# One pool of eight PSUM banks, and the value products of a half step's last four key places moved next to those of the following half step

## The chip, the cores and the metric

The kernel runs on one core of a Trainium2 chip. The metric is the device time of one execution in microseconds; the median of three runs is compared. Its five engines (TensorE, VectorE, ScalarE, GpSimd and SyncE) each work through a queue of their own in order, and wait for each other by semaphores. TensorE multiplies matrices and writes its results to PSUM, which has eight banks here of 128 partitions x 512 float32; VectorE and ScalarE read them from there.

## The reference

The input is x of 8 sequences x 1024 tokens x 256 channels; there are 16 heads of 16 channels. What is computed:

```python
def attn(x):                      # relative positions clipped at +-64
    q, k, v = proj(Wq, bq), proj(Wk, bk), proj(Wv, bv)
    logits = einsum('bhqd,bhkd->bhqk', q, k) + einsum('bhqd,qkd->bhqk', q, embK[idx])
    w = softmax(logits)
    out = einsum('bhqk,bhkd->bhqd', w, v) + einsum('bhqk,qkd->bhqd', w, embV[idx])
    return out @ Wo.T + bo
def ffn(x):                       # weights quantized to -1, 0, 1 by a threshold
    return einsum('bsd,od->bso', x, ternary(weight) * alpha) + bias
x = x + layernorm(attn(layernorm(x)))
x = x + layernorm(ffn(layernorm(x)))
```

## The kernel before

**Work.** The heads are two groups of eight, a sequence is eight tiles of 128 queries: 8 x 2 x 8 = 128 steps, each of one tile of queries and eight heads. A step has two half steps of four heads each (`blk` 0 and 1), four steps are a quad, two steps a pair. For each step the stages are:

- `band_raw` (L902): products of the queries with the table of near positions, four matmuls into one bank. ScalarE copies the bank twice into `praw` (L1403, L1404); SyncE writes that to DRAM (`bs`) and reads it back skewed as `bands`.
- `row_max` (L919), eight times a step: scores for a pair of heads and half of the keys, in two banks, one for each of two heads (the sides). These matmuls have 48 or 51 rows, so two of them share the array as two row tiles. VectorE takes the maximum of either bank, with the band added (L1222) or without (L1216). `max_reduce` and `max_rows` (L929) turn the maxima, which go back by DMA as two more rows of the queries.
- `weights` (L946, with the band added by L950): the logits of four heads at one key place of 128 keys, transposed, in one bank. ScalarE takes the exponential (L1424). The eight key places of a half step are four of kind "X" (the nearest first; they go to `wl`, `wm` and the two of `wr`) and four of kind "Y" (the four of `wy`).
- `weighted` (L970): the products of the values with those weights. A visit is one kind of one half step: four key places x four heads, each with 17 output rows at one of four column tiles, all added up in one bank, `oacc`, over a pair of steps. `merge` (L1245) then joins `wl` and `wm` on VectorE. `out_copy` (L1432) copies `oacc` out after a pair.

Each quad `relative` (L982), `relative_sum` (L995) and `out_norm` (L1006) add the part of the relative values and normalise. The projections of the next sequence (`turn_x`, `project_q`, `far`, `project_k`, `project_v`; L865 to L892) and the output projection, norms and feed forward of finished tiles (`tail_...`, L1020 and L1034) are spread between the steps.

**Banks.** Three banks are the ring of the scores, two the ring of the logits, one is `oacc`, and two are `misc`, which all other stages share. A stage waits on TensorE until the reader of the bank's last user is done.

**Order.** Nothing is scheduled at run time. `timetable()` gives each stage a slot from the table `PLACES` (8 slots a step, 32 a quad; `near` and `rest` are the slots of kinds X and Y in a half step, `value_x` and `value_y` those of their visits). `with_banks()` goes through the slots in order, gives each stage that needs it the `misc` bank that is planned to be free first (`HOLD` is how long each is held, in slots), and moves a stage later where neither is. `order_of()` sorts them for each engine, with the lags of `LAG`; `misc_banks()` turns the plan into the semaphore values that TensorE waits for.

## Time and profile before

| what | before |
|---|---|
| median of three runs | 2571.98 us (2568.47 to 2572.31) |
| the profiled execution | 2569.9 us |
| its span in the trace | 2568.1 us |
| TensorE busy | 2413.4 us, 94% |
| VectorE busy | 2072.1 us, 81% |
| ScalarE busy | 1564.0 us, 61% |
| GpSimd busy | 955.9 us, 37% |
| mean granted TensorE clock | 0.979 |

Times count from the start of the span. A busy TensorE is one with a matmul in flight: matmuls overlap, and a row's length is that of one matmul from issue to end, so rates are read from the starts of rows. "PEld" are the weight loads, which run ahead of the matmuls. A wait stands at the engine that waited, with the instruction that released it.

### The profile page before, as it was taken

The page shows a single profiled execution, that of the slowest core. Times are in us where ns is not written, and L with a number is a line of the kernel's source. Part 1 is how long each engine was busy: PE and PEld are TensorE (multiplying, and loading weights), DVE is VectorE, ACT ScalarE, POOL GpSimd, SP SyncE. Part 2 cuts the span into 40 slices and gives each one's busy share as a digit, 9 for nine tenths or more (in the row PEclk, how much of TensorE's full clock was granted, in tenths as well). Part 3 has the DMA queues.
Part 4 walks back from the last instruction along what each step waited for, and adds up shares of the span by engine and source line. Part 5 has one row for each costly group of instructions (what it writes and reads, how often), then busy time and mean ns, then how long its engine had stood idle before and what let it go on. Part 6 is the DMA issues. An engine that isn't in the chain of part 4 may idle for free.

```text
span 2568.1 us, 101028 instructions
## 1 busy us (share of the span) xinstructions
PE 2413.4 (94%) x41858; PEld 1747.5 (68%) x41858; DVE 2072.1 (81%) x5306; ACT 1564.0 (61%) x2993; POOL 955.9 (37%) x2211
## 2 busy tenths in 40 slices
PE   5499999999999999999999999999999999999995
PEld 4266776777766776767776677676776777676673
DVE  4477779877888878887788878987788877888876
ACT  2266666666666666666666666666666666666651
POOL 3001534435343354425444253433534335442024
PEclk8599999999999999999999999999999999999998
DMA  6856675666746576565756667566774657756510
GB/s 162 228 155 180 184 195 146 167 176 193 205 138 174 165 205 185 148 193 152 206 153 176 184 182 194 147 168 174 199 201 139 173 163 203 192 145 189 153 42 29
DMA packets 696145, 434.20 MB, mean 169 GB/s; under 512 B 215846, under 2 KB 695430, under 8 KB 695558
## 3 DMA queue, kind: packets, MB, share of 16 engines
q1 hardware_dynamic: 695686, 427.75, 60.8%
q8 instruction: 329, 5.39, 0.9%
q14 instruction: 130, 1.06, 0.1%
HBM read 231.91 MB, written 194.92 MB: 166 GB/s over the span
## 4 chain that ended last, share of the span: by engine, by line
PE 54%; DVE 13%; issue 4%; ACT 3%; POOL 1%; DMA 0%; SPq 0%; DVEq 0%; ACTq 0%; POOLq 0%
PE logitsT L946 13%; PE oacc L970 12%; PE scores L919 7%; PE logitsT L950 6%; DVE junk L1222 4%; DVE maxes L1216 4%; PE misc L1034 3%; PE misc L875 3%; PE misc L995 2%; PE misc L892 2%; PE misc L902 1%; ACT wr L1424 1%; PE misc L982 1%; DVE stats L1092 1%; PE misc L1006 1%
## 5 line engine op out<-in xcount | busy, mean ns | idle before, releaser
L946 PE MATMUL logitsT<-qs,ks 98*128 98x128 bf16 (+1 forms) x8192 | 915.7, 221 | 21.8 <-ACT wr L1424 8.8
L1222 DVE CUSTOM_DVE_ANT_1 junk<-scores,bands 128x512 bf16<-128x512 f32 x988 | 679.5, 688 | 216.1 <-PE scores L919 66.7
L1424 ACT ACTIVATE wy<-logitsT 128x512 f32<-128x512 f32 x1024 | 581.4, 597 | 332.3 <-PE logitsT L946 321.1
L946 PEld LDWEIGHTS logitsT<-qs,ks 98*128 98x128 bf16 (+1 forms) x8192 | 562.4, 99 | 274.9 <-issue 150.4
L1216 DVE TENSOR_REDUCE maxes<-scores 128x1 f32<-128x512 f32 x1024 | 656.5, 682 | 93.8 <-PE scores L919 92.5
L919 PE MATMUL scores<-mks,mqs 48*128 48x256 bf16 (+6 forms) x3712 | 448.5, 289 | 36.8 <-DVE maxes L1216 12.6
L1424 ACT ACTIVATE wr<-logitsT 128x512 f32<-128x512 f32 x512 | 305.3, 596 | 200.2 <-PE logitsT L946 191.6
L950 PE MATMUL logitsT<-ident,bands 128*128 128x128 f32 x2048 | 410.6, 278 | 0.0
L1453 POOL TENSOR_SCALAR rs<-rs 128x1 int32<-128x1 int32 (+1 forms) x217 | 48.6, 224 | 803.3 <-DVE rs L1097 793.8
L950 PEld LDWEIGHTS logitsT<-ident,bands 128*128 128x128 f32 x2048 | 293.2, 143 | 20.6
L1458 POOL TENSOR_SCALAR rs<-rs 128x1 f32<-128x1 f32 x744 | 282.7, 383 | 64.9
L970 PE MATMUL oacc<-wy,vs 128*17 128x128 f32 (+1 forms) x9216 | 275.2, 262 | 4.5 <-ACT wy L1424 4.0
L919 PEld LDWEIGHTS scores<-mks,mqs 48*128 48x128 bf16 (+1 forms) x3712 | 138.9, 94 | 196.9 <-DVE maxes L1222 30.2
L1424 ACT ACTIVATE wl<-logitsT 128x512 f32<-128x512 f32 x256 | 158.6, 619 | 154.3 <-PE logitsT L950 152.5
L1463 POOL TENSOR_SCALAR rs<-rs 128x1 f32<-128x1 f32 x744 | 219.6, 298 | 66.1
L970 PEld LDWEIGHTS oacc<-wy,vs 128*17 128x17 f32 x9216 | 206.2, 97 | 53.1 <-issue 34.7
L1403 ACT ACTIVATE praw<-misc 128x512 f32<-128x512 f32 x256 | 154.7, 604 | 40.3 <-DMA bs<-praw 32.5
L1245 DVE COPY_PREDICATED wm<-later,wl 128x512 f32<-128x512 int32 x224 | 171.1, 764 | 0.0
L1424 ACT ACTIVATE wm<-logitsT 128x512 f32<-128x512 f32 x256 | 152.9, 597 | 24.6 <-PE logitsT L950 3.8
L970 PE MATMUL oacc<-wr,vs 128*17 128x128 f32 (+1 forms) x4608 | 159.3, 261 | 0.0
L1404 ACT ACTIVATE praw<-misc 128x512 f32<-128x512 f32 x256 | 157.5, 615 | 0.0
L902 PE MATMUL misc<-bandtab,qs 96*128 96x128 bf16 x1024 | 100.3, 220 | 20.3 <-ACT praw L1404 14.5
(147 smaller groups left out, 2991.3 us busy)
## 6 DMA issues: line engine op xcount, KB each, us to landing
bs<-praw SPq DMA_DIRECT2D x256, 512.0 KB, 4.6
bands<-bs SPq DMA_DIRECT2D x224, 512.0 KB, 4.5
ks<-kd SPq DMA_DIRECT2D x64, 384.0 KB, 4.9
qs<-qd SPq DMA_DIRECT2D x112, 192.0 KB
bands<-bs SPq DMA_DIRECT2D x128, 128.0 KB, 3.3
mks<-kd SPq DMA_DIRECT2D x128, 96.0 KB, 3.8
qd<-qparts SPq DMA_DIRECT2D x60, 192.0 KB, 2.6
kd<-kparts SPq DMA_DIRECT2D x60, 192.0 KB, 2.6
```

Source lines behind the costliest of these rows:

```text
L919: mm = e.matmul(scores[(u + side) % NSCORE][:, c % 512:c % 512 + length], mqs[i][HALF * side:HALF * side + depth, p, :], kk[HALF * side:HA ...
L946: mm = e.matmul(lt[:, j * P:(j + 1) * P], kk[0:depth, SLOT[HB * blk + j], kt * P:(kt + 1) * P], qs[i][0:depth, SLOT[HB * blk + j], :], sta ...
L950: mm = e.matmul(lt[:, j * P:(j + 1) * P], band[v % BRING][:, j, c * P:(c + 1) * P], ident[:], start=False, stop=True, is_transpose=True, s ...
L970: mm = e.matmul(oacc[32 * j:32 * j + VW, o0 + q0:o0 + q1], vs[m_ % VRING][:, int(right), kt, h, :], src, start=first and c == 0, stop=True ...
L1216: e.tensor_reduce(top, sc[:], AX.X, ALU.max).then_inc(row_maxed, 1)
L1222: e.tensor_tensor_reduce(junk[:], sc[:].rearrange("p (a c) -> p a c", a=2), banded, 1.0, LOWEST, ALU.add, ALU.max, top).then_inc(row_maxed, 1)
L1245: e.copy_predicated(right, mask.bitcast(I32), left).then_inc(merged, 1)
L1403: e.activation(dst[:, :, 0:P], src, ACT.Copy)
L1404: e.activation(dst[:, :, P:WIN], src[:, :, P - 1:P].broadcast_to([P, HB, P]), ACT.Copy).then_inc(praw_ready, 1)
L1424: e.activation(dst, src, ACT.Exp).then_inc(exp_ready, 1)
L1458: op = e.tensor_scalar(rs[k][:, 3, x:x + 1], rs[k][:, 2, x:x + 1], rs[k][:, 0, x:x + 1], rs[k][:, 2, x:x + 1], ALU.mult, ALU.mult)
L1463: op = e.tensor_scalar(rs[k][:, 2, x:x + 1], rs[k][:, 3, x:x + 1], 1.5, rs[k][:, 2, x:x + 1], ALU.add, ALU.mult)
```

## The change

- All eight PSUM banks become one pool, `bank0` to `bank7`. The scores (two banks at a time), the logits and the accumulation of the values take theirs from it as the other stages do. `with_banks()` plans them: a stage gets the bank that is planned to be free first; the second side of the scores is held 1.1 slots longer (`HOLD_NEXT`); the bank of the values is held from a pair's first visit to its `out_copy`. TensorE's waits are on the reader of the bank's last user, whichever that is.
- The visit of kind Y of a half step moves from slot 4.12 to slot 5.78, next to the visit of kind X of the following half step (3.5 + 2.3 = 5.8).
- A visit signals after each key place, not once; an exponential that overwrites a buffer waits for that place alone, and `merge` for the first two.
- At the start all eight banks are cleared by VectorE, where it was `oacc` alone.
- Some places, lags and holds have other numbers. The second half's band is now read back ahead of the first's.

```diff
-NLOG, NMISC, NSCORE = 2, 2, 3
+NBANK = 8
...
- 'half': 3.55,
+ 'half': 3.5,
...
- 'near': (0.0, 0.76, 0.72, 0.98),
- 'rest': (1.76, 2.1, 2.5, 2.77),
+ 'near': (-0.38, 0.76, 0.72, 0.98),
+ 'rest': (1.86, 1.98, 2.5, 2.77),
  'value_x': 2.3,
- 'value_y': 4.12,
+ 'value_y': 5.78,
  'merge': 3.2,
- 'out_copy': 7.74,
+ 'out_copy': 9.48,
...
+        if stage == "weighted" and k[0] // 2 in sums:
+            banks = sums[k[0] // 2]
+        elif stage == "out_copy":
+            banks = sums[k[0]]
+            until[banks[0]] = slot + HOLD[stage]
...
-                bank = until.index(min(until))
-                if until[bank] > slot:
+                banks = tuple(sorted(range(NBANK), key=lambda x: until[x])[:2 if stage == "row_max" else 1])
+                free = max(until[x] for x in banks)
+                if free > slot:
...
-         'out_norm': 0.7,
+         'out_norm': 0.24,
...
+HOLD_NEXT = 1.1
+HOLD = {'weighted': 0.0,
+ 'out_copy': 1.0,
+ 'row_max': 0.45,
+ 'weights': 0.45,
...
- 'band_raw': 0.2,
+ 'band_raw': 0.23,
...
-                            pe.wait_ge(row_maxed, u + side - NSCORE + 1)
-                            mm = e.matmul(scores[(u + side) % NSCORE][:, c % 512:c % 512 + length],
+                            pe.wait_ge(*frees[side])
+                            mm = e.matmul(banks[side][:, c % 512:c % 512 + length],
...
-                    pe.wait_ge(exp_ready, block + 1 - NLOG)
+                    pe.wait_ge(*free)
...
-                    mm.then_inc(pvX if kind == "X" else pvY, 1)
+                        mm.then_inc(pvX if kind == "X" else pvY, 1)
...
-            e.memset(oacc[:], 0.0).then_inc(oacc_zeroed, 1)
+            for bank in misc:
+                op = e.memset(bank[:], 0.0)
+            op.then_inc(banks_zeroed, 1)
...
-                    dve.wait_ge(pvX, value["pvX", s, blk])
+                    dve.wait_ge(pvX, value["pvX", s, blk] - 2)
...
-                        act.wait_ge(done, value["pv" + kind, (v - 1) // 2, (v - 1) % 2])
+                        act.wait_ge(done, value["pv" + kind, (v - 1) // 2, (v - 1) % 2] - 3 + c % 4)
```

What stands in a row on TensorE, in the middle of the program. First the kernel before: the end of a half step's key places, its X visit, and the turning of the row maxima.

```order
L946 MATMUL logitsT<-qs,ks 128x128 x8
L919 MATMUL scores<-mks,mqs 128x128 x4
L919 MATMUL scores<-mks,mqs 128x256 x2
L946 MATMUL logitsT<-qs,ks 128x128 x4
L970 MATMUL oacc<-wl,vs 17x128 x4
L970 MATMUL oacc<-wm,vs 17x128 x4
L970 MATMUL oacc<-wr,vs 17x128 x8
L929 MATMUL misc<-ident,negmax 8x128
L946 MATMUL logitsT<-qs,ks 128x128 x8
```

Some ten rows further on, the same kernel's Y visit, between the scores and the next key places:

```order
L919 MATMUL scores<-mks,mqs 128x128 x4
L919 MATMUL scores<-mks,mqs 128x256 x2
L970 MATMUL oacc<-wy,vs 17x128 x16
L946 MATMUL logitsT<-qs,ks 128x128 x5
L950 MATMUL logitsT<-ident,bands 128x128
```

In the changed kernel (its line numbers are 22 higher) the two stand together, the Y visit of one half step ahead of the X visit of the next:

```order
L968 MATMUL bank<-qs,ks 128x128 x4
L941 MATMUL bank<-mks,mqs 128x128 x4
L941 MATMUL bank<-mks,mqs 128x256 x2
L968 MATMUL bank<-qs,ks 128x128 x8
L992 MATMUL bank<-wy,vs 17x128 x16
L992 MATMUL bank<-wl,vs 17x128 x4
L992 MATMUL bank<-wm,vs 17x128 x4
L992 MATMUL bank<-wr,vs 17x128 x8
L951 MATMUL bank<-ident,negmax 8x128
L968 MATMUL bank<-qs,ks 128x128 x8
```

The 16 matmuls with `wy` are no longer between scores and logits; 32 matmuls of one shape stand where 16 stood.

The second place is TensorE's `band_raw` and what follows, here with the numbers of the banks. Before, the raw products are in `misc1`, which no stage takes again until `turn_x`, eleven rows on:

```order
L902 MATMUL misc1<-bandtab,qs4 128x128 x4
L919 MATMUL scores1<-mks1,mqs0 128x256
L919 MATMUL scores2<-mks1,mqs0 128x256
L919 MATMUL scores1<-mks1,mqs0 128x256
L919 MATMUL scores2<-mks1,mqs0 128x256
L970 MATMUL oacc<-wy,vs0 17x64 x32
L919 MATMUL scores0<-mks1,mqs0 128x384
L919 MATMUL scores1<-mks1,mqs0 128x384
L919 MATMUL scores0<-mks1,mqs0 128x128
L919 MATMUL scores1<-mks1,mqs0 128x128
L982 MATMUL misc0<-wm,reltab 32x64 x16
L865 MATMUL misc1<-ident,xc 128x128 x4
```

In the changed kernel, `bank5` has the raw products of a half step, and logits take it again after the scores of one visit:

```order
L924 MATMUL bank5<-bandtab,qs4 128x128 x4
L941 MATMUL bank0<-mks1,mqs2 128x256
L941 MATMUL bank6<-mks1,mqs2 128x256
L941 MATMUL bank0<-mks1,mqs2 128x256
L941 MATMUL bank6<-mks1,mqs2 128x256
L941 MATMUL bank1<-mks1,mqs2 128x512
L941 MATMUL bank7<-mks1,mqs2 128x512
L968 MATMUL bank5<-qs0,ks0 128x128 x4
```

Two groups of scores stand between a bank's use by `band_raw` and its next one, where three groups, a Y visit and relative products stood. The shortest distance is that of 24 of the 161 places where logits follow raw products in a bank.

## Rows read from the trace of the kernel before

**Rows 1.** The page: span, then each engine's busy us, share, instructions.

```profile
span 2568.1 us, 101028 instructions
...
PE 2413.4 (94%) x41858; PEld 1747.5 (68%) x41858; DVE 2072.1 (81%) x5306; ACT 1564.0 (61%) x2993; POOL 955.9 (37%) x2211
```

**Rows 2.** Busy time by window: length; PE, PEld, DVE, ACT, POOL busy; clock, DMA share, GB/s.

```profile
1350.00:1500.00 150.00, 145.73 (x2604) 105.76 (x2601) 126.50 (x327) 96.04 (x182) 58.07 (x141) 1.00 0.61 169
2250.00:2400.00 150.00, 146.14 (x2696) 105.33 (x2688) 130.64 (x337) 97.97 (x183) 41.86 (x116) 1.00 0.58 159
```

**Rows 3.** TensorE's timeline: start us, length of the merged row us, line, operands, count.

```profile
1202.67 0.40 PE L946 MATMUL logitsT<-qs,ks 101*128 101x128 bf16 x4
1203.00 0.40 PE L919 MATMUL scores<-mks,mqs 48*128 48x256 bf16 x4
...
1207.13 0.40 PE L946 MATMUL logitsT<-qs,ks 98*128 98x128 bf16 x4
1207.36 0.39 PE L902 MATMUL misc<-bandtab,qs 96*128 96x128 bf16 x4
...
1209.26 1.07 PE L970 MATMUL oacc<-wy,vs 128*17 128x128 f32 x32
1210.26 0.45 PE L946 MATMUL logitsT<-qs,ks 101*128 101x128 bf16 x5
...
1214.13 0.61 PE L946 MATMUL logitsT<-qs,ks 98*128 98x128 bf16 x8
1214.58 0.39 PE L902 MATMUL misc<-bandtab,qs 96*128 96x128 bf16 x4
```

**Rows 4.** By the tile of the score maxima: who waited for them, us, times.

```profile
  PEld scores L919: 59.4, 147
  PE scores L919: 23.3, 61
```

**Rows 5.** By the exponentials' line: who waited for them, us, times.

```profile
  PEld logitsT L946: 95.7, 395
  PE logitsT L946: 15.3, 58
  PEld oacc L970: 11.3, 31
  PE oacc L970: 4.0, 11
```

**Rows 6.** TensorE's timeline: the idle time before a row is in brackets.

```profile
1211.61 0.83 PE L946 MATMUL logitsT<-qs,ks 101*128 101x128 bf16 x8
1212.69 0.40 PE L946 MATMUL logitsT<-qs,ks 101*128 101x128 bf16 x4 [0.26 <-ACT wr L1424]
```

**Rows 7.** By the tile `praw`: ns min/median/max of one, first and last start us.

```profile
L1403 ACT ACTIVATE praw<-misc x256: 590/605/632, 52.2 to 2444.6; 128x512 f32<-128x512 f32 x128
L1404 ACT ACTIVATE praw<-misc x256: 592/618/645, 52.7 to 2445.1; 128x512 f32<-128x512 f32 x128
```

**Rows 8.** By the line L1222: the score maxima with the band.

```profile
L1222 DVE CUSTOM_DVE_ANT_1 junk<-scores,bands x988: 664/691/696, 79.0 to 2486.0; 128x512 bf16<-128x512 f32 x198
```

**Rows 9.** Timeline of all engines: turned outputs and their second reader.

```profile
1337.46 0.66 PE L1006 MATMUL misc<-ident,oT 128*128 128x128 f32 x4
...
1341.63 0.42 DVE L1279 TENSOR_TENSOR attn<-misc,rsum 128x256 f32<-128x256 f32 x1
```

**Rows 10.** TensorE's timeline at the start of the program.

```profile
27.28 3.62 PE L875 MATMUL misc<-xnT,wq 128*128 128x256 f32 x8 [3.86 <-DVE vs L1195]
...
99.56 0.59 PE L902 MATMUL misc<-bandtab,qs 96*128 96x128 bf16 x4 [10.64 <-ACT praw L1404]
```

**Rows 11.** VectorE's timeline at the start of the program.

```profile
0.92 0.48 DVE L1125 MEMSET oacc<- 128x512 f32 x1 [0.92 <-PEq L1555]
```

## What the change will do to the time

> **What bounds the kernel now.** I read the page's busy shares first, then the windows, then TensorE's timeline, and last the lists of who waited for whom. The page [rows 1] has TensorE busy for 2413.4 of 2568.1 us, VectorE for 2072.1 and ScalarE for 1564.0. The windows [rows 2] have the same picture in the middle of the run: 145.73 of 150 us at a granted clock of 1.00, with VectorE at 126.50, and late in the run at 130.64. So TensorE sets the end, VectorE is second with 16% to spare, ScalarE is far off. An edit pays here only if it shortens TensorE's own queue, and busy time alone hides two kinds of loss in it. They show in the starts of the rows, not in their lengths.
>
> The first loss is the **change of tiling shape**. Four full-size bf16 matmuls followed by another full-size line take 0.23 us from start to start (1207.13 to 1207.36); the same four followed by the two-row-tile scores take 0.33 us (1202.67 to 1203.00) [rows 3]. Each change between full, two-row-tile (scores) and four-column-tile work (values, relative, relative sum, far) costs 0.095 to 0.10 us. A visit of the values to TensorE (16 float32 matmuls, which the trace counts as 32) takes 1.00 us from start to start (1209.26 to 1210.26), of which 0.905 is work.
>
> The second is **waiting for a PSUM bank** (or for weights) in the middle of that queue. Where TensorE should have gone on at 1211.61 + 8 x 0.057 = 1212.07, its next four matmuls start at 1212.69: 0.62 us lost, though the row shows 0.26 idle, since the modelled ends of the matmuls cover the rest [rows 6]. So the idle time of PE rows is a lower bound of such waits, and the idle time of weight loads (PEld) an upper one. Over the run the scores' banks cost between 23.3 and 59.4 us and the logits' banks between 15.3 and 95.7; together 38.6 to 155.1 [rows 4, 5]. The example's factor 0.62/0.26 on 38.6 gives 92; waits that are covered entirely come on top, and I take **110 us**.
>
> **The change, part by part.**
>
> *A. Joined visits.* No matmul is added or removed; the last four places' products move down the queue, to just ahead of the next half step's first four. Counting neighbours in the order of both programs, the values come in 512 separate visits before and in 320 after, and TensorE changes its shape 2942 times before and 2579 times after. It is not 2 x 192 fewer everywhere, since a visit often stood next to scores, where taking it out leaves one change behind, and since other stages moved too. 363 x 0.095 = **-34.5 us**. Bounds: 363 x 0.09 and x 0.10, so 33 to 36. The middle of the run has no cover for this on TensorE, so it counts in full.
>
> *B. Values that wait for their weights.* The values wait for ScalarE's last exponential for 4.0 us by PE rows and 11.3 by PEld rows [rows 5]. After the change the first four places' last logits are followed by at least 1.5 us of other TensorE work ahead of the visit, where before there are places with 0.6; the last four have 2.8 us and more. **-8 us** (-4 to -11).
>
> *C. The ring of three score banks and the ring of two logits banks go.* That gives back up to the 110 us above.
>
> *D. All readers now share the banks, slow ones too.* Each stage takes the bank that the plan thinks was freed longest ago, and TensorE, in order, waits at that place if it was not. A logits bank is now reused after at least 0.87 us of TensorE work when another key place had it, where before one in ten had 0.65 or less: of the logits' waits nearly nothing stays (5 us). A score bank is not better off. Its first side is read in 0.69 us once VectorE comes to it [rows 8], and is taken again after a median of 1.9 us of TensorE work, a quarter of them within 1.35, much as before (1.9 and 1.2): of these waits I keep 40 of some 45 us. New are the slow readers, which had two banks of their own. The band's raw products are read by two activations of 0.605 and 0.618 us, one after the other [rows 7], and with their start and some queue on ScalarE I take 1.5 us; 161 blocks of logits get such a bank, 24 of them after 0.64 us of TensorE work, 24 within 1.1 and 61 after 1.35. 24 x 0.86 + 24 x 0.41 + 61 x 0.15 is 40; the 57 other stages that follow such a bank add some 15, and a wait in one place gives slack to the next: 45 in all. The turned outputs are read late: the reader at 1341.63 ends 4.1 us after the four matmuls that start at 1337.46 have streamed [rows 9]. The plan moves that reader up by 0.46 slots, about 1.1 us (32 slots are four steps, some 76 us), which leaves up to 3.0, and takes such a bank again after 1.67 us of TensorE work where it is tightest: 24 places of 0 to 1.4 us, 0.8 in the mean, 19. Output projections, relative sums and far tables have 30 to 40 more places of 0.5 us: 21. D is 5 + 40 + 45 + 19 + 21 = **+130 us**. Net of C: +20. The bounds are no stall but the old ones on scores (45, net -65) and every such wait taken singly with none shared (188, net +78).
>
> *E. The start.* Seven more bank-wide memsets of 0.48 us stand ahead of VectorE's first work [rows 11], 3.4 us, of which its wait for the first input from HBM covers a part, and loads of constants, for which TensorE's first projection waits in any case, more. Against that, projections no longer wait for VectorE's copy of the values' bank (3.86 us idle at 27.28) [rows 10]. But the first steps hang on a band write queued on SP: TensorE's 10.64 us idle before 99.56 [rows 10]. The same DMAs stand ahead of that write, in another order. **-1 us**, bounds -6 to +6.
>
> *F. Finer semaphore counts.* A visit signals four times where it signalled once, so exponentials can overwrite a place early, and the merge starts before the visit ends. The signals cost nothing that shows: eight matmuls in a row, of which the fourth also signals, take 1214.58 - 1214.13 = 0.45 us, as 8 x 0.057 would [rows 3]. The Trainium skill, "TensorE: Matmul & The Clock Gate", section "Why this matters for your kernels", gives a tail of about 26 ns for each increment when tiles run side by side, which over 1536 more increments would be an estimate of 40 us and would take the gain away. The row here is of full-size matmuls, so it speaks against that but does not exclude it.
>
> **The sum** against the profiled execution: -34.5 - 8 - 110 + 130 - 1 = -23.5, so 2568.1 becomes 2544.6. The run around the span takes 1.8 us, and the median of the runs is 3.9 us above the span: 2544.6 + 3.9 = **2548.5**, say 2548, a gain of 0.9%.
>
> **Rivals.**
>
> *1. The pool gives far more.* ScalarE's order now lets half of the raw copies pass one exponential, and VectorE's order puts the score maxima ahead of other work in many places. If the slow readers are mostly done in time, D is 65 instead of 130 and the time is 2548 - 65 = 2483. For it: ScalarE is 61% busy. Against: 1.22 us of copying does not fit in 0.64 us however early it starts.
>
> *2. Slower: banks held by slow readers.* Each late reader now stops whatever stage comes next, at eight banks' worth of places, and VectorE, busy for 84% of the middle and 87% late in the run [rows 2], gets less slack as TensorE gets faster, so it is late more often. If no wait covers another, D is 188 (scores 60 of it): -34.5 - 8 + 78 - 1 = +34.5, 2606. The point that decides is D at about 152. For it: TensorE's order is fixed and a quarter of the reuses of a first side are within 1.35 us. Against: second sides get 4 us and more in half of the places.
>
> *3. Slower by the gate on ScalarE.* The first exponential of the last four places of the next half step now waits until the joined visit has read the same buffer, typically 0.6 us after its logits are there and up to 1.5. Everything behind it on ScalarE (the second such exponential, sometimes a copy for the tail) waits too, and TensorE for their banks. ScalarE's 39% of free time and the visit's 1.9 us cover it, so I price it at nothing; with the cover gone, 0.3 us at each of 255 visits would make +76: 2624.
>
> *4. Nothing moves.* D near 150 gives back what the joins save: 2567 to 2577.
>
> *5. The signals' tail* as the skill has it: the four signals of every visit delay it; worked out from a row, a delay as large as half a change of shape (0.05) at each of the 3 x 256 signals inside a joined visit is 38 us: 2586.
>
> **How the numbers follow.** Forecast (D between 115 and 145, 2533 to 2563): 0.40. Rival 1: 0.22. Rival 4: 0.11. Rival 2: 0.19. Rival 3: 0.05. Rival 5: 0.03. A difference under 0.2% (5 us) is about what a measurement of this kernel cannot tell from none. Faster is the forecast and rival 1: 0.62; same 0.11; slower 0.27. The range takes in rival 1 down to 2475 and rivals 2 and 5 up to 2606; outside stay half of rival 2, rival 3 and the far part of rival 1.
>
> **What would show each step.** A: rows of the values of 64 matmuls that take 1.81 us of work with one change at either end, and TensorE's loads idle on "issue" before the values in half as many places. C and D: logits waiting for exponentials (PEld 95.7) fall under 20; waits of logits for raw copies and of scores for the turned outputs' readers, which do not exist now, appear, 64 us together. B: the values' waits for exponentials near nothing. E: the first logits block within 6 us of today's. Steady windows would show fewer idle microseconds on weight loads; windows of equal length would hold some 1% more matmuls. Wrong would be: waits on VectorE for score banks twice today's (rival 2), ScalarE idle until the values have been read followed by TensorE waiting for that bank (rival 3), or hardly any wait for a slow reader (rival 1).

## The result and the profile after

The changed kernel takes 2651.73 us (median of four runs, 2645.09 to 2658.27) against 2570.22 before (the median of four runs there too, where 2571.98 was that of three): 1.0316 times as long, 95% interval 1.0301 to 1.0330. Forecast were 2548 us, 0.9% faster, with a range up to 2606. Direction and size were both wrong. The line numbers are 22 higher on TensorE, 26 higher for the exponentials (L1450), 25 for the turned outputs' reader (L1304), and `praw` is copied by L1429 and L1430.

The page of the changed kernel, the same lines as [rows 1]:

```profile
span 2648.8 us, 101803 instructions
...
PE 2387.8 (90%) x41858; PEld 1771.6 (67%) x41858; DVE 2083.4 (79%) x5313; ACT 1529.9 (58%) x2993; POOL 938.7 (35%) x2211
```

Its windows, the same stretches and columns as [rows 2]:

```profile
1350.00:1500.00 150.00, 139.91 (x2568) 102.40 (x2565) 127.98 (x336) 91.30 (x177) 50.66 (x142) 0.99 0.57 159
2250.00:2400.00 150.00, 140.89 (x2543) 103.14 (x2542) 128.60 (x342) 89.15 (x173) 60.37 (x167) 0.99 0.56 158
```

VectorE and ScalarE do much the same work as before. TensorE has lost 5 to 6 us of each 150 where before it was busy for 145.73 and 146.14, and late in the run it fits in 2543 matmuls where it had 2696 (the slower kernel is by then at an earlier point of its work). It is nearly the same work with more holes. Who makes them stands in the list of waits (us in total, times, longest), which answers [rows 4, 5]:

```profile
ACT wy L1450 <- PE bank L992: 308.1, 199, 4.1
...
PEld bank L968 <- ACT praw L1430: 49.8, 107, 1.1
...
PEld bank L941 <- DVE attn L1304: 34.5, 31, 1.7
...
PE bank L941 <- DVE attn L1304: 27.0, 31, 1.6
...
PE bank L968 <- ACT praw L1430: 21.2, 40, 0.7
```

and, by the exponentials' line, who waited for them:

```profile
  PEld bank L968: 34.3, 120
  PEld bank L941: 12.2, 49
```

The logits' waits for exponentials are down, not gone (95.7 became 34.3 on weight loads, where under 20 was foreseen), and now scores and other stages wait for exponentials too (12.2 at the scores). New on top, logits wait for the raw copies, and scores 31 times for the reader of the turned outputs. ScalarE now sits idle 308 us ahead of the exponentials of kind Y until value products are done (L992); before, no exponential waited for them.

One stretch of TensorE's timeline shows more than a wait:

```profile
1768.52 0.39 PE L941 MATMUL bank<-mks,mqs 48*128 48x512 bf16 x1
1769.99 0.39 PE L941 MATMUL bank<-mks,mqs 48*128 48x512 bf16 x1 [1.08 <-DVE attn L1304]
...
1772.13 1.91 PE L992 MATMUL bank<-wy,vs 128*17 128x128 f32 x32
1773.82 0.66 PE L992 MATMUL bank<-wl,vs 128*17 128x128 f32 x8
1774.24 0.59 PE L992 MATMUL bank<-wm,vs 128*17 128x128 f32 x8
1774.66 0.61 PE L992 MATMUL bank<-wr,vs 128*17 128x128 f32 x16
1775.20 0.40 PE L968 MATMUL bank<-qs,ks 98*128 98x128 bf16 x4
```

and its windows (the granted clock is the third number from the right):

```profile
1764.00:1768.00 4.00, 3.85 (x41) 2.60 (x39) 3.90 (x11) 2.87 (x6) 3.01 (x7) 1.00 0.38 84
1768.00:1772.00 4.00, 2.85 (x25) 1.60 (x23) 3.79 (x11) 1.34 (x3) 2.27 (x8) 0.90 0.76 200
1772.00:1776.00 4.00, 4.00 (x75) 2.87 (x74) 1.46 (x6) 1.45 (x3) 0.73 (x1) 0.67 0.51 169
```

The second side of the scores starts 1.47 us after the first, because its bank still belongs to the turned outputs. Some 1.2 us later the clock is down to 1.2 GHz, and the joined visit takes 3.07 us (1772.13 to 1775.20) instead of 1.88 (1236.71 to 1238.59 elsewhere). Leaving out the first 150 and the last 80 us, the changed kernel has 17 such stretches, 68 us in all, each just behind one or more waits of 0.5 to 2.6 us; the kernel before has none there.

**Where the time went, summed.** Instead of idle times I use the starts: each stage's time to the next, less what the same kind takes in its fastest tenth, over that same stretch of the trace, and each excess put down to the semaphore that came last. In the table "banks" are waits for a bank's last reader; "other" is the rest (waits for data, "issue", and what the lower clock adds). "Ch." is the count of changes of tiling shape in the order, "low" that of the low-clock stretches. All but the medians and ratios is read from one traced execution of each kernel; that of tuned_no_join took 9 us less than its median, that of signals_visit 14 us more, the others lie within some 6 us of theirs.

| kernel | median us | ratio, 95% | ch. | banks | of it exps / scores / raw / turned outputs / rest | other | low |
|---|---|---|---|---|---|---|---|
| before | 2570.22 | | 2942 | 156 | 70 / 60 / 0 / 0 / 26 | 18 | 0 |
| changed | 2651.73 | 1.0316 (1.0301-1.0330) | 2579 | 210 | 35 / 42 / 50 / 39 / 45 | 77 | 17 |
| join_old_banks | 2678.28 | 1.0417 (1.0394-1.0441) | 2748 | 264 | 143 / 97 / 0 / 0 / 25 | 45 | 9 |
| old_join_two_wy | 2676.83 | 1.0408 (1.0387-1.0430) | 2748 | 263 | 137 / 100 / 0 / 0 / 26 | 35 | 4 |
| moved_old | 2616.26 | 1.0183 (1.0166-1.0201) | 3013 | 195 | 107 / 62 / 0 / 0 / 26 | 19 | 0 |
| pool_no_join | 2542.45 | 0.9890 (0.9874-0.9905) | 2879 | 106 | 3 / 24 / 0 / 14 / 64 | 53 | 4 |
| moved_pool | 2615.94 | 1.0174 (1.0153-1.0195) | 2868 | 182 | 16 / 33 / 42 / 39 / 52 | 43 | 6 |
| two_wy | 2641.98 | 1.0270 (1.0253-1.0288) | 2579 | 204 | 35 / 39 / 47 / 39 / 45 | 79 | 18 |
| attn_late | 2614.24 | 1.0164 (1.0146-1.0183) | 2579 | 188 | 35 / 59 / 47 / 0 / 48 | 64 | 8 |
| next_early | 2581.33 | 1.0042 (1.0028-1.0056) | 2579 | 155 | 16 / 50 / 28 / 29 / 33 | 74 | 10 |
| two_wy_next | 2586.52 | 1.0063 (1.0042-1.0083) | 2579 | 156 | 16 / 51 / 28 / 29 / 33 | 81 | 15 |
| tuned_join | 2559.92 | 0.9958 (0.9943-0.9973) | 2579 | 138 | 48 / 75 / 6 / 0 / 9 | 64 | 10 |
| pool_no_join_next | 2520.09 | 0.9804 (0.9788-0.9821) | 2879 | 73 | 0 / 20 / 0 / 14 / 39 | 61 | 5 |
| tuned_no_join | 2528.11 | 0.9835 (0.9809-0.9860) | 2808 | 35 | 9 / 19 / 0 / 0 / 7 | 107 | 2 |
| tuned_no_join_x | 2512.55 | 0.9777 (0.9754-0.9800) | 2856 | 39 | 8 / 22 / 0 / 0 / 8 | 90 | 4 |
| signals_visit | 2644.75 | 1.0293 (1.0273-1.0314) | 2579 | 205 | 29 / 43 / 50 / 39 / 45 | 92 | 20 |

Before against changed the account closes: banks +54, other +59, changes of shape -34.5, sum +78.5; the spans differ by 80.7.

### The profile page after: what moved, and what is told of

It reads as the page before. It is cut to its first block, busy times and chain, and to the rows that moved or that the text cites. A ratio compares the mean times of both kernels' runs of the same rounds, so it can differ in the third digit from the quotient of the medians.

```text
span 2648.8 us, 101803 instructions
## 1 busy us (share of the span) xinstructions
PE 2387.8 (90%) x41858; PEld 1771.6 (67%) x41858; DVE 2083.4 (79%) x5313; ACT 1529.9 (58%) x2993; POOL 938.7 (35%) x2211
## 4 chain that ended last, share of the span: by engine, by line
PE 57%; DVE 17%; ACT 9%; issue 8%; DMA 3%; SPq 2%; POOL 1%; DVEq 0%; ACTq 0%; POOLq 0%
PE bank L992 16%; PE bank L968 13%; PE bank L941 7%; PE bank L972 4%; DVE junk L1247 4%; DVE maxes L1241 4%; PE bank L897 4%; PE bank L1056 3%; ACT praw L1430 3%; PE bank L1004 2%; ACT wr L1450 2%; PE bank L914 2%; DVE stats L1114 2%; PE bank L1017 1%; DMA xc<-in_x 1%
## 5 line engine op out<-in xcount | busy, mean ns | idle before, releaser
L968 PE MATMUL bank<-qs,ks 98*128 98x128 bf16 (+1 forms) x8192 | 897.1, 222 | 53.0 <-ACT praw L1430 21.2
L1450 ACT ACTIVATE wy<-bank 128x512 f32<-128x512 f32 x1024 | 565.1, 599 | 559.7 <-PE bank L992 308.1
L1247 DVE CUSTOM_DVE_ANT_1 junk<-bank,bands 128x512 bf16<-128x512 f32 x988 | 679.3, 688 | 185.9 <-PE bank L941 41.3
L1241 DVE TENSOR_REDUCE maxes<-bank 128x1 f32<-128x512 f32 x1024 | 656.5, 682 | 160.5 <-PE bank L941 158.9
L968 PEld LDWEIGHTS bank<-qs,ks 98*128 98x128 bf16 (+1 forms) x8192 | 575.9, 99 | 274.8 <-issue 112.6
L941 PE MATMUL bank<-mks,mqs 48*128 48x256 bf16 (+6 forms) x3712 | 440.6, 291 | 98.7 <-DVE attn L1304 27.0
L972 PE MATMUL bank<-ident,bands 128*128 128x128 f32 x2048 | 410.7, 278 | 0.0
L1450 ACT ACTIVATE wr<-bank 128x512 f32<-128x512 f32 x512 | 310.9, 607 | 46.2 <-PE bank L968 41.7
L972 PEld LDWEIGHTS bank<-ident,bands 128*128 128x128 f32 x2048 | 293.0, 143 | 20.3
L992 PE MATMUL bank<-wy,vs 128*17 128x128 f32 (+1 forms) x9216 | 287.9, 270 | 5.2 <-issue 5.2
L992 PEld LDWEIGHTS bank<-wy,vs 128*17 128x17 f32 x9216 | 216.5, 101 | 38.8 <-issue 17.5
L1450 ACT ACTIVATE wl<-bank 128x512 f32<-128x512 f32 x256 | 157.0, 613 | 103.0 <-PE bank L972 101.9
L1429 ACT ACTIVATE praw<-bank 128x512 f32<-128x512 f32 x256 | 153.5, 599 | 97.8 <-PE bank L924 50.7
L1450 ACT ACTIVATE wm<-bank 128x512 f32<-128x512 f32 x256 | 154.9, 605 | 24.8 <-PE bank L972 18.0
L992 PE MATMUL bank<-wr,vs 128*17 128x128 f32 (+1 forms) x4608 | 163.9, 266 | 0.8 <-issue 0.8
L1430 ACT ACTIVATE praw<-bank 128x512 f32<-128x512 f32 x256 | 154.6, 604 | 0.0
L992 PEld LDWEIGHTS bank<-wr,vs 128*17 128x17 f32 x4608 | 119.3, 100 | 2.3 <-issue 0.9
```

The costliest lines, as they stand in the source:

```text
L941: mm = e.matmul(banks[side][:, c % 512:c % 512 + length], mqs[i][HALF * side:HALF * side + depth, p, :], kk[HALF * side:HALF * side + dept ...
L968: mm = e.matmul(lt[:, j * P:(j + 1) * P], kk[0:depth, SLOT[HB * blk + j], kt * P:(kt + 1) * P], qs[i][0:depth, SLOT[HB * blk + j], :], sta ...
L972: mm = e.matmul(lt[:, j * P:(j + 1) * P], band[v % BRING][:, j, c * P:(c + 1) * P], ident[:], start=False, stop=True, is_transpose=True, s ...
L992: mm = e.matmul(m[32 * j:32 * j + VW, o0 + q0:o0 + q1], vs[m_ % VRING][:, int(right), kt, h, :], src, start=first and c == 0, stop=True, s ...
L1241: e.tensor_reduce(top, sc[:], AX.X, ALU.max).then_inc(row_maxed, 1)
L1247: e.tensor_tensor_reduce(junk[:], sc[:].rearrange("p (a c) -> p a c", a=2), banded, 1.0, LOWEST, ALU.add, ALU.max, top).then_inc(row_maxed, 1)
```

## The experiments

In what follows, "first-half" means the four key places of kind X of a half step (`near`, `value_x`), "second-half" the four of kind Y (`rest`, `value_y`, `wy`); the "second half step" is `blk` 1. "The join" is the visits moved next to each other.

**First question: the join or the pool?** Theory 1 was that slow readers on the shared banks made the loss (rival 2 of the prediction); theory 2 that the joined visit holds up ScalarE's exponentials (rival 3).

*join_old_banks*: the kernel before, with the visits joined but for the last half step of a pair, whose bank is copied out.

```diff
-            at(o + x_["value_y"], "weighted", s, blk, "Y")
+            at(o + (x_["value_y"] if i % 2 and blk else 5.78), "weighted", s, blk, "Y")
```

> The kernel before with the join alone: the second four key places of three half steps in four stand at 5.78 instead of 4.12 (the last half step of a pair keeps 4.12, because its bank is copied out at 7.74), all banks and rings as before. Visits of the values fall from 512 to 352 and changes of TensorE's tiling shape from 2942 to 2748, so the join by itself is worth 194 x 0.095 = 18.4 us. Theory 1 (the loss of the changed kernel is made by banks that slow readers hold, not by the join): faster than before by 5 to 20 us, 2550 to 2565 us, with the waits of logits for exponentials (70 us before) grown by no more than 15 us. Theory 2 (the join gates ScalarE: a second-half exponential waits for the joined visit, and the logits behind it wait for ScalarE): slower than before by 30 us or more, over 2600 us, with the logits' waits for exponentials over 110 us.

*pool_no_join*: the changed kernel with `value_y` 4.12 and `out_copy` 7.74 as before.

```diff
- 'value_y': 5.78,
+ 'value_y': 4.12,
- 'out_copy': 9.48,
+ 'out_copy': 7.74,
```

> The changed kernel without the join: the value products back at 4.12 and the copy of the sums at 7.74, the pool of eight banks and everything else as changed. Changes of tiling shape go from 2579 back to 2879 (+28.5 us). Theory 1 (readers on the shared banks): the waits stay, the visits are split again, so it ends within 20 us of the changed kernel or above it, 2640 to 2690 us, and TensorE still waits some 100 us for the raw products', the turned outputs' and the scores' readers. Theory 2 (ScalarE gated by the joined visit): the gate goes, so 40 us or more come back, under 2610 us.

The join alone costs 107 us on the old banks, where it takes in three visits of four; the pool alone gains 28 (1.1%). Theory 1 as put is wrong on both. And the waits that I had charged to the pool are the join's too: without it the raw copies cost nothing once the steps run (0 against 50 us), and the turned outputs' reader costs 14 us, not 39. In join_old_banks ScalarE is held up as theory 2 says; its waits, and who waited for the exponentials there:

```profile
ACT wy L1424 <- PE oacc L970: 424.1, 192, 4.9
```

```profile
  PEld logitsT L946: 198.9, 629
  PE logitsT L946: 66.4, 153
```

**Second question: is it ScalarE's gate?** A second buffer for the second-half exponentials takes the gate away and leaves every order as it is.

```diff
-        wy = sb("wy", [P, 4, 512])
+        wy = [sb(f"wy{i}", [P, 4, 512]) for i in range(2)]
...
-                    elif c > 1 and v:
-                        act.wait_ge(done, value["pv" + kind, (v - 1) // 2, (v - 1) % 2])
+                    elif c > 1 and v > c // 4:
+                        u = v - 1 - c // 4
+                        act.wait_ge(done, value["pv" + kind, u // 2, u % 2])
```

> The kernel join_old_banks (old banks, the join in three half steps of four, 2678 us) with a second buffer for the second-half exponentials, so that they wait for the visit of the half step before the last one and no longer for the joined visit beside them; nothing else moves. Its trace shows the first and the second of these exponentials 2.38 us after their logits where the kernel before has 0.80 us. Theory 2 (the gate on ScalarE makes the whole cost of the join on the old banks): the two come back to about 0.8 us, the logits' waits for exponentials from 143 to 80 us or less, the scores' waits for maxima from 96 to about 60, and with the 18 us of fewer tiling changes the time is 2545 to 2570 us. Rival (the joined visit itself, 64 matmuls in a row in which VectorE and ScalarE get nothing to do, makes it): still over 2630 us.

> The changed kernel with the same second buffer for the second-half exponentials; the order of every engine and the table of banks stay as they are. Theory 2 (the gate is the cost of the join in the pool as well): the logits' waits for exponentials and those for the raw products, which ScalarE copies, go, and 80 us or more come back: under 2575 us. Theory 3 (in the pool the join costs through the bank table: with the products in the new places other stages draw the banks of slow readers): replaying the table with the ungated latencies of pool_no_join leaves 210 of 213 us of waits, so 2630 to 2655 us.

The gate went: the median time from the last of the first second-half logits to the end of their exponential is 0.80 us again (2.38 in join_old_banks), and no exponential waits for value products any more. The time did not move beyond its uncertainty of some 8 us: 2676.83 and 2678.28. The rival had expected over 2630. Who waited for the exponentials in old_join_two_wy:

```profile
  PEld logitsT L946: 171.3, 506
  PE logitsT L946: 65.5, 144
```

So theory 2 falls on the old banks, and in the pool it is worth about 10 us (2641.98 against 2651.73; with both uncertainties 4 to 16), a small part of 109. The waits for exponentials in the pool stay at 35 us without the gate.

**Third question: what does a visit do where it stands?** The waits grew at a few places. On the old banks the second first-half logits of the second half steps waited 2.1 us in all before and 55.4 with the join. TensorE's timeline there, before:

```profile
1198.85 0.28 PE L950 MATMUL logitsT<-ident,bands 128*128 128x128 f32 x1
1199.05 0.39 PE L919 MATMUL scores<-mks,mqs 48*128 48x256 bf16 x4
1199.38 1.07 PE L970 MATMUL oacc<-wy,vs 128*17 128x128 f32 x32
1200.38 0.70 PE L946 MATMUL logitsT<-qs,ks 101*128 101x128 bf16 x5
```

The same place in join_old_banks:

```profile
1246.63 0.28 PE L950 MATMUL logitsT<-ident,bands 128*128 128x128 f32 x1
1246.84 0.40 PE L919 MATMUL scores<-mks,mqs 48*128 48x256 bf16 x4
1247.17 0.40 PE L946 MATMUL logitsT<-qs,ks 101*128 101x128 bf16 x4
1248.56 0.23 PE L946 MATMUL logitsT<-qs,ks 98*128 98x128 bf16 x1 [1.00 <-ACT wl L1424]
```

The fifth of the logits matmuls at 1200.38 (at 1200.85) takes the bank that was filled up to 1198.85: 2.00 us between. In join_old_banks the same reuse is 1248.56 - 1246.63 = 1.93 us, in moved_old (below) 1218.72 - 1216.70 = 2.02. In this place the reader sets the distance, with or without the visit. Before, the visit of 1.00 us lay inside it and cost nothing; joined, it takes its time elsewhere and the hole stays. That is theory 4, cover.

The place shown is one of the longest. Over all 128 such places the distance from the last product in the bank to the next use is 1.94 us in the mean before, 1.31 in join_old_banks and 1.33 in moved_old. It ends within 0.1 us of the exponential that reads the bank in 7 places before, and in 106 in either of the other two. So the reader is what TensorE waits for once the visit is gone, but of the visit's 1.00 us only some 0.4 was cover here in the mean (55.4 us over 128 places), not all of it.

The rival (theory 5) is that the length of the joined visit starves the readers. *moved_old* moves the same visits without joining them:

```diff
-            at(o + x_["value_y"], "weighted", s, blk, "Y")
+            at(o + (x_["value_y"] if i % 2 and blk else 5.25), "weighted", s, blk, "Y")
```

> The kernel before with the same three visits in four moved as in join_old_banks, but not joined: they stand at 5.25, after the last first-half logits of the next half step and before its first second-half logits, so every visit stays on its own (512 visits). Changes of tiling shape 3013 against 2942, 71 x 0.095 = 6.7 us more. Theory 4 (cover: a visit between two logits or two scores is the 0.9 us of work in which their readers finish; where it is taken from between them TensorE waits, wherever it is put instead): the second first-half logits of the second half steps, which waited 2.1 us in all before and 55.4 us with the join, wait 40 us or more here too, and the time is 2620 to 2680 us. Theory 5 (it is the length of the joined visit, 64 matmuls in a row, that starves the readers): the visits are short again and the time is 2575 to 2595 us.

```profile
1216.70 0.28 PE L950 MATMUL logitsT<-ident,bands 128*128 128x128 f32 x1
1216.91 0.40 PE L919 MATMUL scores<-mks,mqs 48*128 48x256 bf16 x4
1217.24 0.40 PE L946 MATMUL logitsT<-qs,ks 101*128 101x128 bf16 x4
1218.72 0.23 PE L946 MATMUL logitsT<-qs,ks 98*128 98x128 bf16 x1 [1.08 <-ACT wl L1424]
```

The hole is there with the visit merely moved: 56.7 us at this place against 55.4 with the join. The whole costs 46 us: 2616 us, 4 us under the range of theory 4 and 21 us over that of theory 5. A visit on its own covers something in its new place: the first scores of the third pair of heads wait 4.8 us (14.5 before) and the first two second-half logits of the second half steps 2.3 (21.0 before). Merged with its neighbour it gives no such cover: 32.0 and 22.8 us, and another 62 us on the time, though 265 fewer changes of shape save 25. So the hole needs no long visit, and theory 5 falls as its cause. For the merging, the larger part of the 107 us, it does not fall. Two visits apart can cover two waits and one of double length only one, which fits the two places; but no run tells this apart from another effect of 64 matmuls in a row.

*moved_pool* asks the same in the pool (the edit of moved_old on pool_no_join):

> The kernel pool_no_join (2542 us) with three visits in four moved to 5.25 and not joined, the copy of the sums where it was. Changes of tiling shape 2868 (2879 in pool_no_join). A replay of the table of banks with the latencies of pool_no_join gives 201 us of waits, 122 without the move, 210 for the changed kernel. If in the pool the move by itself costs, through cover and through the draw of banks: 2600 to 2640 us, and the scores' waits for the turned outputs' reader go from 14 to about 37 us. If it is the merging of two visits: 2545 to 2575 us.

Moving costs 73 us here (2542 to 2616), inside the range expected for it, and the changed kernel lies 36 us above that, net of the 27 us that 289 fewer changes of shape save. The 36 us are the merging together with the move of the fourth visit and of the copy of the sums. That most of it is the move shows in who is waited for. In moved_pool:

```profile
PEld bank L968 <- ACT praw L1430: 39.0, 67, 1.0
...
PEld bank L941 <- DVE attn L1304: 34.6, 31, 1.7
```

and in pool_no_join, where the first of these lines does not exist:

```profile
PEld bank L941 <- DVE attn L1304: 11.4, 15, 1.1
```

The copies and readers are no slower (the second copy ends a median of 1.46 us after the last raw product's start in both kernels, the turned outputs' reader 1.54 and 1.56 us after their last matmul's start); the stages that reuse their banks come sooner. How much of the 73 us is cover and how much another draw of banks stays open.

**Fourth question: the planner's holds.** The plan hands out banks by guesses of how long a reader needs. I replayed the bank table of a kernel with TensorE's own work and the reader latencies of a trace; for the changed kernel the replay gives 213 us of waits, 37 of them for the turned outputs, where the trace has 210 and 39.

*attn_late* (`'out_norm': 0.75` to `1.6`) and *next_early* (`HOLD_NEXT = 1.1` to `0.3`) change one number each of the changed kernel; *two_wy_next* and *pool_no_join_next* are next_early's number on two_wy and pool_no_join.

> The changed kernel with one other number changed: the bank of the turned outputs counts as taken for 1.6 slots instead of 0.75, about the 3.5 us that its reader took in a quarter of the cases. Of the waits of the changed kernel this takes away those of the scores for that reader (31 of 1.0 to 1.6 us, 39 us in all), which stood ahead of most of the 17 falls of the granted clock. Theory 1 by the replay: 213 to 182 us of waits, so 2620 us if the clock's falls stay, 2595 to 2605 us if most of them go too (they cost about 28 us). If the falls have another cause than these waits, their number stays at 12 or more. Theory 2: 2640 us or more.

> The changed kernel with one number of the bank planner changed: the second bank of a score stage counts as taken 0.3 slots longer than the first, not 1.1 (a slot is about 2.4 us; the trace of the changed kernel has the second bank's maximum 0.64 us after the first's). More banks are then on offer at each draw, and fewer stages follow a slow reader. Theory 1, refined (the planner's wrong figures for how long readers hold a bank decide who waits for whom): replaying the new bank table with the reader latencies of the changed kernel's trace takes TensorE's waits from 213 to 132 us, so 2555 to 2590 us, and more if the falls of the granted clock go with them. Theory 2 (ScalarE's gate) or a cost of the joined visits themselves: no more than 15 us, 2635 to 2655 us.

> The kernel two_wy with the planner's figure for a score stage's second bank at 0.3 as in next_early (2581 us). Theory 3: the table decides, and the replay gives 144 us of waits, so 2550 to 2585 us, within 20 us of next_early. Theory 2: the gate and the table both cost, so it comes in at 2500 to 2530 us.

> The kernel pool_no_join (2542 us) with the same figure at 0.3. Replayed with the latencies of pool_no_join the table's waits fall from 122 to 73 us. If it is the table of banks that decides in the pool, 2485 to 2510 us, the fastest so far; if pool_no_join has already nothing left to gain from the table (its waits being those for exponentials and turned maxima that no bank cures), 2530 us or more.

attn_late gives 37 us back: the 39 us of waits for that reader go, 17 us of new ones on scores come, the low-clock stretches fall from 17 to 8; the time lies between the two figures expected. next_early gives 70 back with a single number, as the replay said (2555 to 2590): a second score bank counted as taken 1.1 slots (2.6 us) longer than the first, where the trace has 0.64 us, kept banks out of the draw and sent others to slow readers. The gate is worth nothing here (two_wy_next 2586.52, next_early 2581.33). pool_no_join_next came in at 2520.09, 22 us better than pool_no_join where the replay gave 48: direction right, size not.

*tuned_no_join* and *tuned_join* have all holds fitted in that replay, each for its own order: the first without the join and with `value_x` 2.4 and `value_y` 4.22, the second with the places of the changed kernel. Three lines of the edit of tuned_no_join (tuned_join has `HOLD_NEXT` 0.3 and the same 1.4):

```diff
- 'value_x': 2.3,
+ 'value_x': 2.4,
...
-HOLD_NEXT = 1.1
+HOLD_NEXT = 0.5
...
- 'out_norm': 0.75,
+ 'out_norm': 1.4,
```

> The pool without the join (pool_no_join_next, 2520 us) with the planner's holds fitted in a replay of the bank table, mainly those of slow readers raised to what their readers take (turned outputs 1.4 slots, relative products 0.6, relative sums 0.5, turned maxima 0.5, attention rows' products 1.15, key projections 0.93), the score stage's second bank 0.5 after the first, and the values' products 0.1 slots later. The replay leaves 39 us of waits against 91 (latencies of pool_no_join_next); the two steps replayed so far came out at 0.45 and 0.8 of what the replay gave. So 2475 to 2500 us; 2515 us or more if the table has nothing left to give.

> The same fit for the pool with the join (next_early, 2581 us): the replay leaves 104 us of waits against 151. So 2535 to 2560 us. By theory 4 a fitted table can't make up for the cover that the join takes, and it stays 40 us or more above tuned_no_join; if the join costs only through the table it was given, it ends within 10 us of tuned_no_join or below it, since it has 229 fewer changes of tiling shape (22 us).

tuned_no_join missed: bank waits fell to 35 us, the time rose from 2520 to 2528, which is hardly more than the uncertainty. A new wait stands in its list:

```profile
PEld bank L951 <- DVE negmax L1254: 64.5, 66, 3.5
```

where pool_no_join_next has

```profile
PEld bank L951 <- DVE negmax L1254: 8.1, 20, 3.6
```

The 0.1 slots had moved the first-half visit behind the turning of the maxima, which till then had it as cover:

```profile
1185.15 0.27 PE L951 MATMUL bank<-ident,negmax 128*8 128x128 f32 x1 [0.81 <-DVE negmax L1254]
1185.36 0.41 PE L992 MATMUL bank<-wl,vs 128*17 128x128 f32 x8
```

*tuned_no_join_x* puts `value_x` back to 2.3:

> The kernel tuned_no_join (2528 us) with one number back: the first-half visits at 2.3 instead of 2.4. At 2.4 they stood behind the transpose that turns the row maxima (2.32 in odd places), and that transpose waited 59.9 us in all for VectorE's reduction of the maxima, where pool_no_join_next with the visit ahead of it waits 2.7. Theory 4 (cover): the wait falls under 5 us; the visits' own waits for exponentials grow by some 3 us, the changes of tiling shape by 48 (5 us): 2470 to 2490 us. If the wait had another cause, 2520 us or more.

```profile
PEld bank L924 <- DMA qs<-qd: 19.7, 22, 1.9
PEld bank L968 <- DMA qs<-nm: 18.9, 15, 2.8
...
PEld bank L951 <- DVE negmax L1254: 13.3, 20, 3.5
```

The wait is gone but for 7.8 us by the starts, and the time is 2512.55, 2.2% faster than before and the fastest of all. It is above the 2470 to 2490 expected. Waits for DMAs have grown (the loads of the queries and of the maxima into them, 10.5 and 8.1 us in pool_no_join_next), perhaps because TensorE moves on faster; no run tested that. tuned_join ends at 2559.92. It is faster than before by 0.4%, the best with the join, 47 us above tuned_no_join_x and 32 above tuned_no_join. Theory 4 had asked for 40 or more against the latter, the other reading for 10 or less; neither was met, and the join stays dearer under either fitted table.

**Last: the finer signals.** *signals_visit* is the changed kernel with one increment of 4 for each visit:

```diff
-                        mm.then_inc(pvX if kind == "X" else pvY, 1)
+                    mm.then_inc(pvX if kind == "X" else pvY, 4)
```

> The changed kernel with the values' products signalled once per visit and kind again, by an increment of 4 on the last matmul of the visit where the change has one increment of 1 on the last matmul of each key place; 512 increments instead of 2048. The prediction put the finer signals at nothing. If that holds: 2640 to 2662 us, at most a few us slower because ScalarE's first second-half exponential waits for the whole visit. If each increment costs TensorE 0.026 us or so, 40 us faster, 2612 us. The Trainium skill, TensorE: Matmul & The Clock Gate, section Why this matters for your kernels, has about 26 ns for each increment; that would be the 40 us.

2644.75 against 2651.73, each with an interval of some 5 us: 1536 increments fewer are worth between nothing and a dozen us. In signals_visit the exponentials of kind Y also wait longer for the visit (455 us of ScalarE idle against 308), which may hide a little more. A tail of the full 40 us of rival 5 is excluded by the time, unless those waits cost nearly as much, against which speaks that all of the gate was worth about 10 us (two_wy); a small tail is not excluded.

## Why the prediction was wrong

- **A, the joined visits (-34.5).** The changes of shape fell as counted, and a joined visit takes 1.88 us, two visits' work and one change. The step that failed is the sentence behind the sum: "The middle of the run has no cover for this on TensorE, so it counts in full." It asked what covers the change of shape, and never what the visit itself covers. The visit at 1209.26 in [rows 3] lies between scores and logits, and I counted its 1.00 us as the same cost wherever it stands. Moved and merged it costs +107 us net on the old banks, 46 by the move and 62 by the merging, and +109 in the pool. On the old banks the waits for banks grow by 108 us over 192 moved visits, 0.56 us for each, against 0.095 for a change of shape.
- **B (-8).** By the starts the values' waits for exponentials went from 4.1 to 6.5 us; on weight loads from 11.3 to 8.8. Nothing. The longer distance to the first four went with exponentials that come later (the first of a half step starts a median of 1.68 us after its first matmul, before 1.18).
- **C (-110).** By the starts the two rings had cost 130 us (70 and 60): right, a bit low.
- **D (+130).** It measured 184 (210 less the 26 that `misc` had cost). Scores 42 (40 foreseen), raw products 50 (45), the rest 19 (21) were right. Waits for exponentials were 35, not 5, and part of them at scores and other stages, which the term left out. They are not the gate's (35 in two_wy too); most stand behind first-half exponentials (13.6 us behind `wl`, whose exponential is the one that starts after 1.68 us), and 0.87 us of TensorE work does not cover that. The turned outputs were 39, not 19: 31 places of 1.3 us, not 24 of 0.8. Rival 2, "D is 188", has this sum, and its point of decision (152) was passed; its time, 2606, was still 46 us too low.
- **Left out altogether:** +59 us of other waits, of which the lower clock explains about 28 (the excess inside the 17 stretches) and "issue" idle of TensorE, 16. [rows 2] had the clock at 1.00, and I took it as given.
- **E (-1).** Right: the first exponential starts at 114.6 us, before at 114.7.
- **F (0).** Right within a dozen us, as far as signals_visit can tell.
- **The rivals.** Rival 2 gave the mechanism with the wrong author: the same pool without the join waits 106 us for banks. Rival 3 was visible to the letter (ScalarE idle until the values are read, 308 us) and nearly free: about 10 us of 109. Rival 1's 2483 was reached by no kernel; the nearest, at 2512 to 2520 us, are without the join. The prediction priced the pool and the join in one sum. Measured apart they are -28 for the pool and +109 for the join.

## What to carry to other kernels

On an engine that works in order, a block of work has two values: its length, and the waits of others that it lies in. Before moving or merging it, ask for the distance between the two uses of each buffer on either side, and for how long the reader takes. What the reader would need beyond the distance without the block is cover, and it comes back as a wait when the block goes. And a gain per merged block (here 0.095 us of shape change) must be held against the cover of the whole block (here some 0.4 us at one place and 0.56 us of bank waits for each moved visit, of 1.0 us), not against nothing. Where a planner deals out shared buffers, its guesses of how long readers hold them can be worth more than the sharing (28 us here): one of them, four times too long, was 70 us.

## What the hardware showed

- The granted clock fell to 1.2 GHz in a TensorE that is busy for 90% of the run, after single waits of 1.1 us idle (1.47 us from start to start) and once after two of 0.55 and 0.63 us. 17 stretches of 68 us in all cost about 28 us on top of the waits that led to them; taking away 31 such waits (attn_late) left 8 stretches. With as many waits over 1 us on the old banks (44 in join_old_banks, some 43 in the changed kernel) there were 9 stretches, so the length of one wait alone does not tell.
- ScalarE idle for 308 us in a wait that was not there before (for L992) cost about 10 us; taking away 424 us of such idle time on the old banks, or the wait in next_early, gave back nothing that can be measured.
- "Issue" idle of up to 2.6 us ahead of 13 single TensorE rows appears in the changed kernel, 16 us in all (before, 0.8 us in 2 rows); other kernels of the pool have some 5 to 17 us of it after the start. Nothing in the profile explains it, and it stays open.
